# Zero products on TensorE in two places where it stands still, in an RWKV and SwiGLU block

## Chip, cores and metric

One core of one Trainium2 chip runs the kernel. The metric is the device time of one execution in microseconds. The kernel before takes 332.64 us (median of 3 runs).

## What is computed

The input x is 4096 steps of 256 channels, float32.

```python
xx = shift_by_one_step(x)
xk, xv, xr = (x * mix + xx * (1 - mix) for the three mixes)
k, v = xk @ Wk.T, xv @ Wv.T
rwkv = sigmoid(xr @ Wr.T) * wkv(-exp(time_decay), time_first, k, v)   # a recurrence over the steps
x = layernorm(x + rwkv @ Wo.T)
h = silu(x @ w_gate.T / 127) * (x @ w_up.T / 127)                     # 768 hidden, integer weights
x = layernorm(x + h @ w_down.T / 127)
```

## The kernel before, in words

The steps are cut into NC = 9 chunks, 0 to 8: 512 steps each, the first and the last 256. Channels lie on the partitions, in CH = 2 halves; the 768 hidden channels are NM = 6 tiles of 128. Work goes in rounds. Round j does the recurrence and the output product of chunk j, the projections K, V and R of chunk j+1, and the feed-forward of chunk j-1. Rounds 1, 2, 7 and 8 are written out, and rounds 3 to 6 are a hardware loop. The order on each engine is written out by hand, and engines wait for each other by semaphores.

TensorE's order in a round (`round_`, from L1038 on) is: gate and up products of chunk j-1 (`gate_up`, L1011, results in bank_a and bank_b), its down product (`down`, L1034, into bank_a), then the output product of chunk j (`attention_out`, L979, into bank_b), the projections K (bank_a) and V (bank_d) of the next chunk (`project`, L969), the transposes of x1 (`transpose_x1`, L988) and the projection R (bank_c). The feed-forward stands twice in the code, once for small and once for large weights, behind a branch on `any_wide`; only the first is run here, and the jump over the second comes right before the output product. In round 1 the projection V of chunk 2 comes earlier, in the middle of the down product of chunk 0. In round 8 the output product stands between the third and the fourth sixth of the down product of chunk 7, inside the branch.

`down` takes its six tiles in order. Tile m waits for `hhi` (ACT, L498) and `hlo`, the low part of the hidden tile; for tiles 0 to 3 POOL makes that (L344), for tiles 4 and 5 DVE (`low_part`, L763). DVE's order late in a round is: hidden products (L755), low part of tile 4, `gate_num` (L693), low part of tile 5, `divide` (L702, writes `rwkv` and lets the output product start), then `residual2` (L771) and its statistics (L709), then per half of the chunk the attention residual `res1` (L722, reads bank_b, so it waits for the output product) and statistics (L709), the means (L714), and the running maximum of the next chunk (L614).

`num_parts` counts `num_new` (L673), by which DVE has read V of chunk j from bank_d. From there on bank_d is free until the next V projection.

`keep_warm(bank, times)` (L941) multiplies a 128x128 tile of zeros with a 128x256 one and drops the result in the first 256 columns of a bank. The kernel before has it at the start (4 times), in round 0 (4 and 2 times, bank_a) and in round 8 (2 times, bank_c). A float32 product is two matmul records in the trace: `keep_warm(bank, 4)` is 8, and the output product of a full chunk (4 row blocks by 2 halves) is 16 at L979. A product in down's fp32r is one record.

Of the kernel before, what the change touches and what calls it, by code (L numbers as in the profile page):

```python
# [14 lines left out]
def rwkv_swiglu_kernel(nc: bass.Bass, xT: bass.AP, x: bass.AP, params: bass.AP, wk: bass.AP, wv: bass.AP,  # L15
# [14 lines left out]
    NM = H // P  # L30
# [19 lines left out]
    with ctx:  # L50
# [3 lines left out]
        def ps(name, shape):  # L54
            return ctx.enter_context(nc.psum_tensor(name, shape, f32))

        def sem(name):
            return ctx.enter_context(nc.semaphore(name))
# [74 lines left out]
        bank_d = ps("bank_d", [P, 2, N])  # L133
# [57 lines left out]
        num_parts = sem("num_parts")  # L191
# [36 lines left out]
        def first(c):  # L228

            return isinstance(c, int) and c == 0  # L230

        def last(c):
            return isinstance(c, int) and c == NC - 1

        def steps(c):

            return N // 2 if isinstance(c, int) and c in (0, NC - 1) else N
# [14 lines left out]
        def halved(c):  # L252

            return N // steps(c)
# [681 lines left out]
        def _(pe):  # L936
            def keep_warm(bank, times):


                for _ in range(times):  # L940
                    nc.tensor.matmul(bank[:, 0, 0:C], zeros[:, 0:P], zeros[:, :], start=True, stop=True)  # L941
# [29 lines left out]
                    mm.then_inc(ready, 1)  # L971

            def attention_out(c):
                pe.wait_ge(rwkv_ready, c + 1)
                if not first(c):
                    pe.wait_ge(hid_ready, c * NM)
                for q in range(steps(c) // P):
                    for h in range(CH):
                        mm = nc.tensor.matmul(attn[:, q, :], rwkv[:, h, q * P:(q + 1) * P], woT[:, h, :],  # L979
                                              start=(h == 0), stop=(h == CH - 1))  # L980
                    if q % 2 == 1:
                        mm.then_inc(attn_ready, halved(c))
# [33 lines left out]
            def down(c, tiles, full):  # L1016
                w = wd_f if full else wd_r
                if 0 in tiles:
                    if last(c):
                        pe.wait_ge(res2_ready, c * 2)  # L1020
                    else:
                        pe.wait_ge(act_ready, c * NM + NM)
                for m in tiles:
                    pe.wait_ge(hhi_ready, c * NM + (m + 1))
                    if m < NP:
                        pe.wait_ge(hlo_ready, c * NP + (m + 1))
                    else:
                        pe.wait_ge(hlo_last_ready, c * (NM - NP) + (m - NP + 1))
                    for q in range(steps(c) // P):
                        for part in (hhi, hlo):  # L1030


                            hp = part[:, m, q * P:(q + 1) * P]
                            mm = nc.tensor.matmul(ffn[:, q, :], hp.bitcast(f32) if full else hp, w[:, m, :],  # L1034
                                                  start=(m == 0 and q % 2 == 0 and part is hhi),
                                                  stop=(m == NM - 1 and part is hlo), skip_group_check=True)
                        if m == NM - 1 and q % 2 == 1:
                            mm.then_inc(ffn_ready, halved(c))  # L1038

            def ffn_products(j, full):  # L1040

                if full:
                    pe.wait_ge(ffn_w_f32_ready, 3)
                gate_up(j - 1, range(2), full)
                gate_up(j - 1, range(2, NM), full)
                if last(j):
                    down(j - 1, range(NM // 2), full)
                    attention_out(j)
                    down(j - 1, range(NM // 2, NM), full)
                elif isinstance(j, int) and j == 1:  # L1050
                    down(0, range(3), full)
                    project(2, V)
                    down(0, range(3, NM), full)
                else:
                    down(j - 1, range(NM), full)

            def round_(j, ffn, nxt):
# [9 lines left out]
                if not last(j):  # L1067
                    attention_out(j)
# [77 lines left out]
```

## Time and profile before

| | |
|---|---|
| runs, us | 332.36, 332.64, 334.7 |
| median, us | 332.64 |
| the profiled execution, us | 333.28 |
| its span in the profile, us | 331.4 |
| mean granted TensorE clock | 0.929 |
| PE busy | 286.2 us (86%) |
| DVE busy | 286.5 us (86%) |
| ACT busy | 215.5 us (65%) |
| POOL busy | 162.4 us (49%) |

The span runs from the first to the last instruction in the profile, and the time of the execution is 1.9 us longer. PE is TensorE's matmuls, PEld its weight loads. Matmuls are pipelined, so records of neighbours overlap: a matmul of a dense stream is shown longer than its distance to the next. The granted clock is a share of full speed (2.4 GHz). The rows speak of the executions' own time, in us from the start of the span.

### The profile page before, as it was taken

Reading aid. Unit: us, or ns where it says so; the run is one execution under the profiler, and the core shown is the slowest. Engines: PE = TensorE matmul, PEld = TensorE weight load, DVE = VectorE, ACT = ScalarE, POOL = GpSimd, SP = SyncE. Lnnn points to the kernel's source line nnn. Section 1 sums busy time; section 2 is a strip of 40 time slices with the busy share of each in tenths; the row PEclk is TensorE's granted clock in tenths of the full one; section 3 lists DMA queues with packets and bytes.
Section 4 is the critical chain, followed back from the end, with each engine's and each line's share of the span. In section 5 each row is a group of like instructions: output and inputs, shape, how many; then the busy total and the mean of one; then the engine's idle time right before and its main releaser. Section 6 shows DMA issues by size and latency. Waiting matters only on the chain.

```text
span 331.4 us, 4458 instructions
## 1 busy us (share of the span) xinstructions
PE 286.2 (86%) x1250; PEld 209.3 (63%) x1250; DVE 286.5 (86%) x484; ACT 215.5 (65%) x384; POOL 162.4 (49%) x125
## 2 busy tenths in 40 slices
PE   7686779999679994999969997999969995999892
PEld 5333666567655783747855677657855684868782
DVE  5999798899869989499888998999889998589764
ACT  3587467396816886088943888288934986099375
POOL 2567445407970199303991079703991099006030
PEclk9989679999969999699969999899979999899998
DMA  7701200400013010210104001030103010101002
GB/s 260 279 0 63 66 1 2 128 1 33 2 22 107 2 64 4 71 56 0 63 0 127 0 16 47 11 116 0 63 0 95 1 65 2 34 1 63 2 5 97
DMA packets 13527, 16.32 MB, mean 49 GB/s; under 512 B 704, under 2 KB 11200, under 8 KB 13504
## 3 DMA queue, kind: packets, MB, share of 16 engines
q1 hardware_dynamic: 12816, 15.48, 14.5%
q10 hardware_dynamic: 688, 0.53, 0.5%
q8 instruction: 15, 0.25, 0.3%
q14 instruction: 8, 0.07, 0.1%
HBM read 11.81 MB, written 4.19 MB: 48 GB/s over the span
## 4 chain that ended last, share of the span: by engine, by line
DVE 34%; PE 30%; issue 19%; ACT 13%; DVEq 1%; ACTq 0%
PE bank_b L979 12%; PE bank_b L1011 5%; DVE rwkv L702 5%; DVE hid L755 5%; PE bank_a L1011 5%; DVE wts L631 4%; DVE pmax L614 3%; ACT L514 3%; DVE state L660 3%; DVE state L648 2%; ACT den L454 2%; ACT den L460 2%; DVE gap L621 2%; PE bank_a L969 2%; DVE kv L654 2%
## 5 line engine op out<-in xcount | busy, mean ns | idle before, releaser
L344 POOL TENSOR_TENSOR hlo<-hid,hhi 128x512 fp32r<-128x512 f32 (+1 forms) x36 | 47.2, 1313 | 141.9 <-ACT hhi L498 141.9
L329 POOL TENSOR_TENSOR mix<-mix,xt 128x512 f32<-128x512 f32 (+1 forms) x46 | 59.9, 1333 | 9.3 <-ACT mix L424 9.3
L1034 PE MATMUL bank_a<-wd_r,hhi 128*128 128x256 f32 x192 | 48.8, 293 | 13.3 <-DVE hlo L763 13.3
L979 PE MATMUL bank_b<-woT,rwkv 128*128 128x256 f32 x128 | 40.8, 486 | 9.7 <-issue 6.9
L1034 PE MATMUL bank_a<-wd_r,hlo 128*128 128x256 f32 x192 | 47.4, 286 | 0.0
L1034 PEld LDWEIGHTS bank_a<-wd_r,hhi 128*128 128x128 f32 x192 | 36.9, 192 | 16.5 <-issue 15.6
L474 ACT ACTIVATE lnv<-mv,eps 128x4 f32<-128x4 f32 (+1 forms) x18 | 5.2, 290 | 58.7 <-DVE mv L714 58.7
L979 PEld LDWEIGHTS bank_b<-woT,rwkv 128*128 128x128 f32 x128 | 31.5, 253 | 17.9 <-issue 10.8
L498 ACT ACTIVATE hhi<-hid 128x512 fp32r<-128x512 f32 (+1 forms) x54 | 31.1, 578 | 11.2 <-DVE hid L755 11.1
L1034 PEld LDWEIGHTS bank_a<-wd_r,hlo 128*128 128x128 f32 x192 | 37.1, 193 | 0.3 <-issue 0.2
L416 ACT ACTIVATE wts<-wts 128x512 f32<-128x512 f32 (+1 forms) x54 | 28.1, 580 | 9.5 <-DVE wts L631 9.5
L1011 PE MATMUL bank_a<-x1hi,wg_r 128*128 128x512 f32 (+1 forms) x96 | 32.1, 414 | 1.5 <-ACT act L490 0.9
L424 ACT ACTIVATE mix<-dx,par 128x512 f32<-128x512 f32 (+1 forms) x46 | 28.6, 682 | 6.5 <-POOL dx L323 6.5
L490 ACT ACTIVATE act<-bank_a 128x512 f32<-128x512 f32 (+1 forms) x48 | 27.3, 568 | 7.0 <-PE bank_a L1011 6.4
L755 DVE TENSOR_TENSOR hid<-bank_b,act 128x512 f32<-128x512 f32 (+1 forms) x48 | 30.7, 642 | 1.3 <-PE bank_b L1011 0.6
L969 PE MATMUL bank_a<-mix,wkT 128*128 128x512 f32 (+1 forms) x64 | 28.9, 596 | 2.9 <-POOL mix L329 2.9
L1011 PE MATMUL bank_b<-x1hi,wu_r 128*128 128x512 f32 (+1 forms) x96 | 29.7, 391 | 1.5 <-DVE hid L755 1.5
L1011 PE MATMUL bank_a<-x1lo,wg_r 128*128 128x512 f32 (+1 forms) x96 | 29.7, 387 | 0.2
L1011 PE MATMUL bank_b<-x1lo,wu_r 128*128 128x512 f32 (+1 forms) x96 | 29.2, 386 | 0.0
L969 PE MATMUL bank_d<-mix,wvT 128*128 128x512 f32 (+1 forms) x64 | 27.2, 567 | 0.9 <-POOL mix L329 0.9
L969 PE MATMUL bank_c<-mix,wrT 128*128 128x512 f32 (+1 forms) x64 | 27.2, 566 | 0.0
L660 DVE TENSOR_TENSOR_SCAN state<-wts,state,kv 128x512 f32<-128x512 f32 (+1 forms) x18 | 26.3, 1466 | 0.0
(105 smaller groups left out, 581.6 us busy)
## 6 DMA issues: line engine op xcount, KB each, us to landing
xt<-xT SPq DMA_DIRECT2D x7, 513.0 KB, 3.9
xrow<-x SPq DMA_DIRECT2D x7, 512.0 KB, 3.9
out<-y SPq DMA_DIRECT2D x6, 512.0 KB, 2.8
wg_i<-wg SPq DMA_DIRECT2D x1, 768.0 KB, 8.9
wu_i<-wu SPq DMA_DIRECT2D x1, 768.0 KB, 10.3
wd_i<-wd SPq DMA_DIRECT2D x1, 768.0 KB, 12.0
out<-y SPq DMA_DIRECT2D x3, 256.0 KB, 2.1
xt<-xT SPq DMA_DIRECT2D x2, 257.0 KB, 3.1
```

The lines of the kernel that those rows point to most:

```text
L329: nc.gpsimd.tensor_tensor(mix[:, i, h, 0:n], mix[:, i, h, 0:n], xt[:, h, 0:n], ALU.add).then_inc(mixed, share(c, i, h))
L344: nc.gpsimd.tensor_tensor(hlo[:, m, 0:n], hid[:, m % NH, 0:n], hhi[:, m, 0:n].bitcast(f32), ALU.subtract).then_inc(hlo_ready, 1)
L416: nc.scalar.activation(wts[:, i, h, 0:n], wts[:, i, h, 0:n], ACT.Exp, scale=-1.0 if i == IN_OLD else 1.0).then_inc(wts_ready, 1)
L424: nc.scalar.activation(mix[:, i, h, 0:n], dx[:, h, 0:n], ACT.Copy, scale=par[:, MIX + i, h:h + 1]).then_inc(dx_scaled, share(c, i, h))
L490: nc.scalar.activation(act[:, m % 2, 0:n], gate_bank(c)[:, m % 2, 0:n], ACT.Silu, scale=SCALE).then_inc(act_ready, 1)
L498: nc.scalar.activation(hhi[:, m, 0:n], hid[:, m % NH, 0:n], ACT.Copy).then_inc(hhi_ready, 1)
L660: nc.vector.tensor_tensor_scan(state[:, 0, h, 1:n + 1], wts[:, IN_OLD, h, 0:n], kv[:, h, 0:n], state[:, 0, h, 0:1], ALU.mult, ALU.add).the ...
L755: nc.vector.tensor_tensor(hid[:, m % NH, 0:n], up_bank(c)[:, m % 2, 0:n], act[:, m % 2, 0:n], ALU.mult).then_inc(hid_ready, 1)
L969: mm = nc.tensor.matmul(bank[:, d, 0:n], w[:, h, d * P:(d + 1) * P], mixed_x[:, i, h, 0:n], start=(h == 0), stop=(h == CH - 1))
L979: mm = nc.tensor.matmul(attn[:, q, :], rwkv[:, h, q * P:(q + 1) * P], woT[:, h, :], start=(h == 0), stop=(h == CH - 1))
L1011: mm = nc.tensor.matmul(bank[:, m % 2, 0:steps(c)], w[:, h, m * P:(m + 1) * P], xp, start=(h == 0 and part is x1hi), stop=(h == CH - 1 and ...
L1034: mm = nc.tensor.matmul(ffn[:, q, :], hp.bitcast(f32) if full else hp, w[:, m, :], start=(m == 0 and q % 2 == 0 and part is hhi), stop=(m ...
```

## The change

`attention_out` of chunks 1 to 7 now first waits until bank_d is free and makes four zero products into it. `down` of chunks 1 to 7 does the same with three ahead of its last tile. Nothing is removed or moved.

```diff
             def attention_out(c):
+                if not first(c) and not last(c):
+                    pe.wait_ge(num_parts, c + 1)
+                    keep_warm(bank_d, 4)
                 pe.wait_ge(rwkv_ready, c + 1)
                 if not first(c):
                     pe.wait_ge(hid_ready, c * NM)
...
                 for m in tiles:
+                    if m == NM - 1 and not last(c) and not first(c):
+                        pe.wait_ge(num_parts, c + 2)
+                        keep_warm(bank_d, 3)
                     pe.wait_ge(hhi_ready, c * NM + (m + 1))
                     if m < NP:
                         pe.wait_ge(hlo_ready, c * NP + (m + 1))
```

## Rows read from the trace of the kernel before

**Rows 1.** The page, busy tenths and granted clock in 40 slices.

```profile
PE   7686779999679994999969997999969995999892
...
PEclk9989679999969999699969999899979999899998
```

**Rows 2.** Waits: engine, tile, line, whom for, us in total, times, longest.

```profile
PE bank_a L1034 <- DVE hlo L763: 13.3, 6, 2.8
PE bank_b L979 <- issue: 6.9, 3, 2.7
...
DVE res L722 <- PE bank_b L979: 16.7, 13, 3.3
```

**Rows 3.** Timeline of TensorE in round 4: start, duration, what, count, idle before.

```profile
165.47 0.28 PE L1034 MATMUL bank_a<-wd_r,hlo 128*128 128x256 f32 x1
168.01 0.36 PE L1034 MATMUL bank_a<-wd_r,hhi 128*128 128x256 f32 x1 [2.26 <-DVE hlo L763]
...
169.19 0.41 PE L1034 MATMUL bank_a<-wd_r,hlo 128*128 128x256 f32 x1
170.22 6.25 PE L979 MATMUL bank_b<-woT,rwkv 128*128 128x256 f32 x16 [0.61 <-DVE rwkv L702]
```

**Rows 4.** Timeline of DVE in round 4.

```profile
167.78 2.30 DVE L702 TENSOR_TENSOR rwkv<-num,den 128x1024 f32<-128x1024 f32 x1
...
171.21 1.39 DVE L709 BATCH_NORM_STATS2 stats<-res 128x6 f32<-128x256 f32 x4
...
174.83 0.75 DVE L709 BATCH_NORM_STATS2 stats<-res 128x6 f32<-128x256 f32 x2
176.51 0.69 DVE L722 TENSOR_TENSOR res<-bank_b,xrow 128x512 f32<-128x512 f32 x1 [0.92 <-PE bank_b L979]
```

**Rows 5.** Windows: stretch, length, busy of PE, PEld, DVE, ACT, POOL, clock, DMA.

```profile
170.22:175.30 5.08, 5.08 (x12) 4.09 (x13) 3.54 (x9) 0.30 (x1) 5.08 (x5) 0.50 0.00 0
...
308.61:310.25 1.64, 1.64 (x8) 1.46 (x9) 1.15 (x2) 0.20 (x1) 0.00 (x0) 1.00 0.00 0
```

**Rows 6.** Windows at the end of down, rounds 2, 7 and 4; last number GB/s.

```profile
90.50:91.70 1.20, 0.80 (x4) 0.51 (x3) 1.20 (x2) 1.20 (x3) 1.20 (x2) 0.50 0.05 14
...
278.80:280.30 1.50, 0.20 (x2) 0.00 (x0) 1.50 (x3) 0.47 (x2) 1.50 (x2) 1.00 0.05 11
169.20:170.20 1.00, 0.41 (x2) 0.11 (x1) 1.00 (x2) 1.00 (x3) 1.00 (x1) 0.50 0.00 0
```

**Rows 7.** Timeline of TensorE: down and output product of rounds 1 to 7.

```profile
56.34 0.28 PE L1034 MATMUL bank_a<-wd_r,hlo 128*128 128x256 f32 x1
57.11 3.72 PE L979 MATMUL bank_b<-woT,rwkv 128*128 128x256 f32 x16 [0.49 <-DVE rwkv L702]
...
93.09 5.56 PE L979 MATMUL bank_b<-woT,rwkv 128*128 128x256 f32 x16 [1.78 <-issue]
...
131.96 6.60 PE L979 MATMUL bank_b<-woT,rwkv 128*128 128x256 f32 x16 [2.67 <-issue]
...
205.93 0.40 PE L1034 MATMUL bank_a<-wd_r,hhi 128*128 128x256 f32 x1 [2.27 <-DVE hlo L763]
...
208.14 4.38 PE L979 MATMUL bank_b<-woT,rwkv 128*128 128x256 f32 x16 [0.32 <-DVE rwkv L702]
...
241.97 0.36 PE L1034 MATMUL bank_a<-wd_r,hhi 128*128 128x256 f32 x1 [2.27 <-DVE hlo L763]
...
242.88 0.28 PE L1034 MATMUL bank_a<-wd_r,hlo 128*128 128x256 f32 x1
244.19 5.11 PE L979 MATMUL bank_b<-woT,rwkv 128*128 128x256 f32 x16 [1.04 <-DVE rwkv L702]
...
281.48 5.25 PE L979 MATMUL bank_b<-woT,rwkv 128*128 128x256 f32 x16 [2.48 <-issue]
```

**Rows 8.** Timeline of TensorE at the end of down in round 8.

```profile
313.15 0.28 PE L1034 MATMUL bank_a<-wd_r,hlo 128*128 128x256 f32 x1
314.51 1.13 PE L941 MATMUL bank_c<-zeros 128*128 128x256 f32 x4 [1.08 <-issue]
```

## The prediction, made before the changed kernel was run

> **What bounds the kernel now.** I read the waits first, then one round in order of time, then the clock. The page's PEclk line shows what the change is aimed at: TensorE runs below full clock once in most rounds, though the PE line above it is nearly solid [rows 1]. The waits put two holes on TensorE: 13.3 us in 6 rounds ahead of the last sixth of the down product (for DVE's hlo, L763), and 6.9 us of "issue" in just 3 rounds ahead of the output product, L979. The reader is to see also whom this hurts: DVE waits 16.7 us in all for L979's bank_b [rows 2].
>
> Round 4 shows the mechanism. The first five sixths of down end at 165.6, the last eight matmuls come at 168.01 when hlo is there; the last of them takes 0.41 us, where the one before the hole took 0.28: the clock has fallen. rwkv is done at 170.08 (167.78 + 2.30), the output product starts at 170.22 and takes 6.25 us for 16 matmuls [rows 3, 4]. Its first twelve ran at granted clock 0.50, the lower level of 1.2 GHz, at 5.08/12 = 0.423 us each; eight in round 8 ran at 1.00 (2.4 GHz) in 1.64 us, 0.205 each [rows 5]. Round 1's sixteen took 3.72 [rows 7], so that is the full-clock price. DVE needs residual, statistics and one half of the attention residual first, and would be free for the second half at 171.21 + 1.39 + 0.69 + 0.75 = 174.04; it starts it at 176.51, when bank_b is complete [rows 4]. From there on TensorE is dense until five sixths of the next down, and DVE is dense beside it, so a later L979 makes the round later by as much: in rounds 4 to 6 the starts of L979 are 170.22, 208.14, 244.19, distances 37.92 and 36.05; the difference of 1.87 is that of the durations, 6.25 and 4.38 [rows 3, 7]. So what counts is **when the output product ends**, in rounds 1 to 7.
>
> **Rounds 2, 3 and 7** differ. There L979 starts 1.78, 2.67 and 2.48 us after TensorE fell idle, for "issue": nothing in the data is late [rows 7]. Just there stretches of 1.20 and 1.50 us hold DMA traffic of 14 and 11 GB/s, about 16 KB each (the first and the last of the three), while the same place of round 4 has 0 [rows 6]. These are the rounds written out (2 and 7) and the first pass of the loop (3); rounds 4 to 6, which run code that has been run, have none. I take the hole for instruction fetch at the jump over the unused branch of the product code. The new matmuls ahead of L979 stand behind that jump, so they can't run inside the hole. The Trainium skill, "Runtime: NRT & Kernel Launch", section "Instruction fetch mechanics", speaks against the change more strongly: code comes in blocks of 16 KiB, a taken branch to a block not held waits for it, and "The IRAM is only 2 cache lines". By that last sentence each pass of the loop would fetch too, rounds 4 to 6 would do as badly as 2, 3 and 7, and the sum below would be some 6 us higher, an estimate. The trace doesn't agree: in round 4 L979 follows rwkv by 0.14 us and nothing is fetched, so the rows decide.
>
> **The change, part by part.** Per product call keep_warm issues two matmuls: the four calls ahead of L979 are 8, the three ahead of the last sixth are 6. Price of one: L979's, same shapes. Eight cost 8 x 0.205 = 1.65, call it 1.7 us, at full clock and 8 x 0.423 = 3.4 us at half; six cost 1.3 or 2.5. The waits on num_parts are met early (num_new comes three hidden products before), so they cost nothing; queued behind them on TensorE is only what would wait for hlo or rwkv. bank_d is read by nobody then, except in round 1, where it already holds the next V; that alters values, not times. Each place in turn:
>
> Six ahead of the last sixth, rounds 2 to 7: they fill 1.3 us of holes of 13.3/6 = 2.2 us on average, so they end before hlo comes; cost 0. Where the cover is gone, in round 8, they cost their own time.
> In round 8 the last sixth of down(7) follows dense work and no hole is before it: TensorE goes from the last matmul at 313.15 to the old dummies at 314.51, again over an "issue" hole [rows 8]. Everything slides by 1.3. Bounds: 0 (if the slide is taken up by that hole) and 1.3; nearest is the second, since the jump itself comes later.
>
> Eight ahead of L979, **round 1**: last down matmul starts at 56.34, so dummies run from 56.46 to 58.16 [rows 7] and L979 starts at 58.16, not 57.11. The clock was full before. Loss 1.05, all visible, as DVE waits for L979 there.
>
> **Rounds 4 to 6.** Round 4: the last sixth starts at 168.01 and at full clock takes 1.03 (as in round 6, 241.97 to 242.88 plus 0.12); dummies to 170.74, 0.52 later than L979 starts now; L979 then takes 3.72 as in round 1 and ends at 174.46 instead of 176.47: gain 2.0. DVE's 174.04 is earlier, so it doesn't cut this. Round 5: 205.93 + 1.03 + 1.7 + 3.72 = 212.38 against 212.52: gain 0.15. Round 6: 241.97 + 6.45 = 248.42 against 244.19 + 5.11 = 249.30: gain 0.9. Sum 3.05. It rests on the clock staying full: the hole ahead of its fall in round 4 shrinks from 2.26 to about 1 us; if it fell all the same, see D.
>
> **Rounds 2, 3, 7**: L979 now starts at 93.09, 131.96, 281.48 and takes 5.56, 6.60, 5.25: 1.84, 2.88, 1.53 more than 3.72. At half clock half the time is lost, so it ran low for 3.7, 5.8 and 3.1 us. With the change dummies start at those times and 1.7 + 3.72 = 5.4 us of full-clock work follow. The hole between the last sixth and the dummies stays (1.8 to 2.7 us), so the clock can fall in it. Ends: clock full throughout, 5.4 each, changes of -0.15, -1.2, +0.15, sum -1.2; the same loss as now, 1.7 more each, sum +5.1. I take 2.8 us of low clock, a bit under the shortest of the three, since the six dummies ahead keep the clock up to the hole and the fall should come once and later: 5.4 + 1.4 = 6.8, changes +1.25, +0.2, +1.55, sum +3.0.
>
> Sum: +1.05 + 3.0 - 3.05 + 1.3 = +2.3 us. The profiled execution took 333.28 (span 331.4 and 1.9 around it), so 335.6; it stands 0.64 above the median of 332.64, which gives **334.9 us** as median, +0.7%. A measurement of this kernel tells about 1%, or 3.3 us, from no change.
>
> **Rivals.**
> A, slower: the clock loss in the fetch rounds stays whole. The place is the hole ahead of the dummies in rounds 2, 3, 7; the price 1.7 us each on top of today's; it decides once the low clock there lasts over about 4.5 us. Sum +1.05 + 5.1 - 3.05 + 1.3 = +4.4, median 337.0; were all three like round 3 (5.8 low), 8.3 each against 17.4 now, +7.5 and 339.4. For: the clock fell in or just after these holes each time. Against: the earlier hole is now filled.
> B: the clock stays full in all rounds but the dummies are still behind the fetch: +1.05 - 1.2 - 3.05 + 1.3 = -1.9, median 330.7. For: two thirds of the idle time ahead is filled. Against: 1.8 us and more stay empty.
> C, faster: the dummies hide in the issue holes, because the fetched block comes before them or the added code moves the jump targets so that the fetch is early. L979 starts as now and at full clock: -1.84 - 2.88 - 1.53 = -6.25 in place of +3.0, sum -6.95, median 325.7. Against: the jump precedes them, and moved targets can as well put a fetch where none is (round 1, about +2).
> D: it doesn't do what it says: zeros don't hold the clock, so rounds 4 to 6 stay low. Then 8 dummies of 3.4 us push L979 by 2 to 3 us each: about +7 in place of -3.05 on the forecast's sum, +12, median 344. Against: the kernel's own dummies of zeros are followed by full clock, as at 314.51, where four take 1.0 us up to the transposes.
>
> **Chances.** Forecast 0.52 (own range 333 to 336.5), A 0.23, B 0.13, C 0.09, D 0.03. The range 330.5 to 337.5 holds the forecast, B and most of A. Faster by over 1% (below 329.3): C and little else, 0.10. Slower by over 1% (above 336.0): A, D and the upper edge of the forecast, 0.28. Within 1%: 0.62.
>
> **What would show it.** Right: 14 more short matmuls on L941 per round, bank_d; rounds 4 to 6 have PEclk full from down through projection, L979 at 3.6 to 3.8 us, 35.7 us apart; DVE's wait for bank_b under 0.5 us there; in rounds 2, 3, 7 a hole of issue now in front of L941, and L979 starting 1.7 us or more after it; L979 of round 1 about 1 us later; transposes of round 8 1.3 us later relative to the output product. Wrong: L941 right behind the last sixth in rounds 2, 3, 7 with no hole (C); low clock in rounds 4 to 6 (D); L979 in the three fetch rounds at full clock (B) or at 6 us and more behind 3 us of dummies (A).

## The result, and the profile after

The changed kernel takes 336.42 us (median of 4 runs, 334.98 to 337.85) against 332.50 for the kernel before in the same comparison: a ratio of 1.012, 95% interval 1.008 to 1.016. It is slower, by 1.2%. The profiled execution took 335.70 us.

In round 1 the zeros land in bank_d while it holds V of chunk 2: the changed kernel computes with zeros in the first 256 steps of that V's first half, and so do the two runs below that keep these zeros (the output product alone, and all zeros without the branch). The same instructions run either way, but no run tests whether the values touch the times.

The granted clock of the changed kernel in 40 slices, from its page:

```profile
PEclk9899679999979999799999999999999998999998
```

Against [rows 1] the dips of rounds 4, 5 and 6 are gone. What was bought with it is in the waits:

```profile
DVE res L722 <- PE bank_b L982: 16.9, 9, 4.8
...
PE bank_d L941 <- issue: 6.6, 3, 2.2
...
PE bank_a L1040 <- DVE hlo L763: 5.4, 5, 1.5
```

The columns are those of [rows 2]. The wait for hlo fell from 13.3 to 5.4 us, as the zeros lie inside it. The three issue holes are all there, 6.6 us, now in front of the zeros (L941). And what counts up to round 8, DVE's wait for bank_b, is 16.9 us where it was 16.7 [rows 2]: fewer waits, but a longest of 4.8. (Lines move with the diff: L979 is now L982, L1034 is L1040.)

The timeline of TensorE, from the changed kernel. Round 1:

```profile
56.30 1.89 PE L941 MATMUL bank_d<-zeros 128*128 128x256 f32 x8
58.02 3.62 PE L982 MATMUL bank_b<-woT,rwkv 128*128 128x256 f32 x16
```

rwkv was done at 56.96 in this round (55.73 + 1.23). The output product waits for the zeros until 58.02. Round 4:

```profile
167.67 1.46 PE L941 MATMUL bank_d<-zeros 128*128 128x256 f32 x6
170.10 0.36 PE L1040 MATMUL bank_a<-wd_r,hhi 128*128 128x256 f32 x1 [0.97 <-DVE hlo L763]
...
171.09 1.89 PE L941 MATMUL bank_d<-zeros 128*128 128x256 f32 x8
172.81 3.62 PE L982 MATMUL bank_b<-woT,rwkv 128*128 128x256 f32 x16
```

This is the change as meant: 3.62 us for L982 where it was 6.25 [rows 3], at the price of a start 0.6 us behind rwkv. Rounds 5 and 6 look the same. Rounds 2, 3 and 7:

```profile
93.80 3.39 PE L941 MATMUL bank_d<-zeros 128*128 128x256 f32 x8 [2.20 <-issue]
97.03 3.62 PE L982 MATMUL bank_b<-woT,rwkv 128*128 128x256 f32 x16
133.52 3.13 PE L941 MATMUL bank_d<-zeros 128*128 128x256 f32 x8 [2.25 <-issue]
136.44 4.20 PE L982 MATMUL bank_b<-woT,rwkv 128*128 128x256 f32 x16
279.82 2.69 PE L941 MATMUL bank_d<-zeros 128*128 128x256 f32 x8 [2.15 <-issue]
282.30 4.66 PE L982 MATMUL bank_b<-woT,rwkv 128*128 128x256 f32 x16
```

In rounds 3 and 7 the product itself is a little longer too, 4.20 and 4.66 us. Two windows of round 2 tell where the low clock went there; the columns are those of [rows 5]:

```profile
93.80:96.60 2.80, 2.80 (x7) 2.26 (x8) 1.21 (x4) 0.00 (x0) 2.80 (x3) 0.50 0.02 6
97.03:100.40 3.37, 3.37 (x17) 2.98 (x16) 1.31 (x3) 0.00 (x0) 0.96 (x1) 1.00 0.29 77
```

The zeros ran at half clock and the output product at full clock. The zeros took the low clock in the product's place, at 3.2 us to save 1.9 ([rows 7], 5.56 against 3.62). Read in steps of half a microsecond, the granted clock is low for 3.4 us in each of the three rounds. In round 2 this starts in the hole, at 93.2; in rounds 3 and 7 only when zeros already run, at 134.2 and 281.0, and it reaches into the product.

The ledger by rounds: the start of DVE's second L722 of each round, which comes behind its waits for the output product, in both profiled executions, and by how much the distance from the entry above it grew.

| | before, us | after, us | grew by | forecast |
|---|---|---|---|---|
| round 1 | 60.87 | 61.67 | +0.80 | +1.05 |
| round 2 | 98.68 | 100.68 | +1.20 | +1.25 |
| round 3 | 138.60 | 140.68 | +0.08 | +0.2 |
| round 4 | 176.51 | 176.47 | -2.12 | -2.0 |
| round 5 | 212.56 | 212.25 | -0.27 | -0.15 |
| round 6 | 249.35 | 248.02 | -1.02 | -0.9 |
| round 7 | 286.76 | 287.00 | +1.57 | +1.55 |
| round 8, its only L722 | 310.74 | 310.96 | -0.02 | |
| round 8, transposes | 315.48 | 316.87 | +1.17 | +1.3 |
| end of the last instruction of DVE | 328.83 | 330.39 | +0.17 | |
| end of the span | 331.4 | 333.9 | +0.9 | |

Up to the L722 of round 8 the changed kernel is 0.22 us longer, which is about what DVE's wait for bank_b grew by (16.7 to 16.9). The transposes of round 8 add 1.17. The last two rows, +0.17 and +0.9, are outside the forecast: the products behind the transposes, which the change leaves alone, and the final store. So 1.4 of the 2.5 us between the two spans lie where the change acts.

### The profile page after: what moved, and what is told of

It is laid out like the page before. It is cut to its first block, busy times and chain, and to the rows that moved or that the text cites. A ratio compares the mean times of both kernels' runs of the same rounds, so it can differ in the third digit from the quotient of the medians.

```text
span 333.9 us, 4658 instructions
## 1 busy us (share of the span) xinstructions
PE 298.3 (89%) x1348; PEld 221.2 (66%) x1348; DVE 286.6 (86%) x484; ACT 215.2 (64%) x384; POOL 162.3 (49%) x125
## 4 chain that ended last, share of the span: by engine, by line
PE 36%; DVE 32%; issue 17%; ACT 11%; DVEq 1%; ACTq 0%
PE bank_b L982 7%; PE bank_b L1014 5%; PE bank_d L941 5%; PE bank_a L1040 5%; DVE hid L755 5%; PE bank_a L1014 5%; DVE wts L631 4%; DVE pmax L614 3%; DVE state L660 3%; DVE state L648 2%; ACT L514 2%; DVE gap L621 2%; PE bank_a L969 2%; PE bank_d L969 2%; DVE kv L654 2%
## 5 line engine op out<-in xcount | busy, mean ns | idle before, releaser
L1040 PE MATMUL bank_a<-wd_r,hhi 128*128 128x256 f32 x192 | 47.8, 289 | 5.5 <-DVE hlo L763 5.4
L1040 PE MATMUL bank_a<-wd_r,hlo 128*128 128x256 f32 x192 | 46.0, 279 | 0.0
L1040 PEld LDWEIGHTS bank_a<-wd_r,hhi 128*128 128x128 f32 x192 | 36.0, 188 | 9.9 <-issue 9.0
L1040 PEld LDWEIGHTS bank_a<-wd_r,hlo 128*128 128x128 f32 x192 | 36.1, 188 | 0.3 <-issue 0.2
L941 PE MATMUL bank_d<-zeros 128*128 128x256 f32 x98 | 26.9, 421 | 6.6 <-issue 6.6
L982 PE MATMUL bank_b<-woT,rwkv 128*128 128x256 f32 x128 | 30.8, 395 | 0.3 <-DVE rwkv L702 0.3
L982 PEld LDWEIGHTS bank_b<-woT,rwkv 128*128 128x128 f32 x128 | 25.7, 201 | 4.9 <-DVE rwkv L702 0.5
```

## The experiments

Each ran beside the kernel before, on one chip; the first three below and the one with four zero products ahead of the jump shared its runs (median 333.14 us), so did the last two (333.49), and so did the other four (333.59). Where two runs are compared, their ratios to the kernel before are the safer measure. In these texts "one branch" means that only the variant of the feed-forward that is run is left in the program, without the jump; the variant for large weights is missing.

### One place at a time

The zeros ahead of the last sixth alone:

```diff
             def attention_out(c):
-                if not first(c) and not last(c):
-                    pe.wait_ge(num_parts, c + 1)
-                    keep_warm(bank_d, 4)
                 pe.wait_ge(rwkv_ready, c + 1)
```

> The three zero products ahead of the last sixth stay, the four ahead of the output product go. Theory (the loss sits in the eight matmuls ahead of the output product wherever they start late: round 1 and the three rounds with an issue hole): the six matmuls lie inside the wait for hlo and cost nothing in rounds 2 to 7, the output product starts within 0.2 us of rwkv in rounds 4 to 6 and at full clock, round 8 still loses 1.2. Against the kernel before 330.5 us, 2 us faster (328.5 to 332), some 5 under the changed kernel. Rival (six matmuls are too few to hold the clock, and the gain of rounds 4 to 6 came from the eight): output product in rounds 4 to 6 at 4.4 to 6.3 us as before, time 333.5 to 334.

Measured: 331.65 us, ratio 0.995 (0.991 to 1.000). The output product of rounds 4 to 6 in that kernel:

```profile
169.59 5.40 PE L979 MATMUL bank_b<-woT,rwkv 128*128 128x256 f32 x16 [1.04 <-DVE rwkv L702]
...
206.67 3.72 PE L979 MATMUL bank_b<-woT,rwkv 128*128 128x256 f32 x16 [1.04 <-DVE rwkv L702]
...
242.06 3.71 PE L979 MATMUL bank_b<-woT,rwkv 128*128 128x256 f32 x16 [1.04 <-DVE rwkv L702]
```

In rounds 5 and 6 the product runs at full speed with the six matmuls alone; in round 4 it takes 5.40, so the clock still fell there. Of the rounds with an issue hole it is at full speed in round 7 (3.69 us) and not in rounds 2 and 3 (6.10 and 5.36). The time lies within the expected range, but the clock wasn't held in all of rounds 4 to 6 as expected. The first place is nearly free and a little good. The slower half of the change must be the other one:

```diff
                 for m in tiles:
-                    if m == NM - 1 and not last(c) and not first(c):
-                        pe.wait_ge(num_parts, c + 2)
-                        keep_warm(bank_d, 3)
                     pe.wait_ge(hhi_ready, c * NM + (m + 1))
```

> The four zero products ahead of the output product stay, the three ahead of the last sixth go. Theory: the hole ahead of the last sixth is open again, the clock falls as before in rounds 2 to 7, and eight matmuls at 0.42 us (3.4 us in all) stand in front of the output product: rounds 4 to 6 lose 1 to 3 us each instead of gaining; round 8 loses nothing. 338 to 341 us, slower than both kernels. Rival (the eight hold the clock by themselves, and the six only cost): output product at 3.6 us in rounds 4 to 6, 334 to 335 us.

Measured: 338.85 us, ratio 1.017 (1.007 to 1.027). Round 5 of that kernel:

```profile
208.55 0.38 PE L1037 MATMUL bank_a<-wd_r,hhi 128*128 128x256 f32 x1 [2.27 <-DVE hlo L763]
...
210.22 2.86 PE L941 MATMUL bank_d<-zeros 128*128 128x256 f32 x8
212.92 3.62 PE L982 MATMUL bank_b<-woT,rwkv 128*128 128x256 f32 x16
```

The hole of 2.27 us is back, the clock falls, and the eight zeros take 2.7 us up to the product. The product is then at full speed, but that is no gain: the low clock is served in front of it. DVE's wait for bank_b is 23.7 us. Round 4 of the same kernel is different: there the eight zeros ran at full clock without the six (1.7 us up to the product, which took 3.62). By the times the two places simply add up: 0.995 x 1.017 is 1.012, the ratio of the changed kernel. What the first does for the second shows in rounds 5 and 6, where the eight zeros take 1.7 us behind the six and 2.7 or 2.8 without them.

### What the issue holes are

```diff
             def round_(j, ffn, nxt):
                 if ffn:
-                    with pe.If(any_wide == 0):
-                        ffn_products(j, False)
-                    with pe.Else():
-                        ffn_products(j, True)
+                    ffn_products(j, False)
```

The last products, behind the rounds, are written once in the same way, and the load of `any_wide` goes.

> The kernel before, with TensorE's feed-forward products written once, without the branch on any_wide (the variant for large weights is left out; it is not run on these inputs). Theory (the issue holes of rounds 2, 3 and 7 are instruction fetch at the jump over the unused branch): they vanish, the output product follows rwkv by 0.1 to 0.3 us in all rounds, and the end comes 5 to 8 us earlier: 325 to 328. Rival (the hole is something else that comes with first-time code or with the product itself): holes of 1.8 to 2.7 us stay in rounds 2, 3 and 7, 332 to 333.

Measured, on the kernel without any of the new zeros: 325.96 us, ratio 0.975 (0.966 to 0.983). Its output products of rounds 2, 3 and 7:

```profile
92.19 5.39 PE L979 MATMUL bank_b<-woT,rwkv 128*128 128x256 f32 x16 [0.96 <-DVE rwkv L702]
...
129.24 5.40 PE L979 MATMUL bank_b<-woT,rwkv 128*128 128x256 f32 x16 [1.04 <-DVE rwkv L702]
...
277.35 3.72 PE L979 MATMUL bank_b<-woT,rwkv 128*128 128x256 f32 x16 [0.40 <-DVE rwkv L702]
```

No hole of issue is left: the idle time before them now ends with rwkv. The part of the page on DMA queues agrees, for the kernel before and for this one:

```profile
q8 instruction: 15, 0.25, 0.3%
```

```profile
q8 instruction: 6, 0.10, 0.1%
```

Nine packets of 16 KB less. The packets are counted for the whole program; with the traffic inside two of the holes [rows 6] they say that the holes are instruction fetch at the jump. Holes and the low clock behind them cost the kernel before some 7 us. With all zeros of the changed kernel on top of this edit:

> The changed kernel, with TensorE's feed-forward products written once (the variant for large weights is left out; it is not run on these inputs). Theory (without the jump there is no fetch hole, so the zero products do in all rounds what they do in 4 to 6): rounds 2, 3 and 7 have full clock throughout and L979 at 3.6 us about 0.5 us behind rwkv, rounds 1 and 8 lose 1 us each as before. 320 to 324 us; against the same kernel without zeros (325.96) 1 to 2% faster, where with the branch the zeros cost 1.2%. Rival (the eight matmuls cost their length wherever they stand, the fetch has no part in the loss): they again cost about as much as they bring, 326 to 330 us.

Measured: 321.28 us, ratio 0.964 (0.959 to 0.970). The same diff that costs 1.2% with the jumps brings 1.0% without them by the two ratios (0.964 against 0.975), or 1.4% by the medians, which are of different sets of runs (321.28 against 325.96). The two intervals just overlap, so the gain is likely and its size is not sure. Round 3 of this kernel is a good round, 0.6 us behind rwkv and at full clock:

```profile
127.21 1.89 PE L941 MATMUL bank_d<-zeros 128*128 128x256 f32 x8
128.93 3.62 PE L982 MATMUL bank_b<-woT,rwkv 128*128 128x256 f32 x16
```

### The same zeros on the other side of the jump

```diff
             def attention_out(c):
-                if not first(c) and not last(c):
-                    pe.wait_ge(num_parts, c + 1)
-                    keep_warm(bank_d, 4)
...
-                    if m == NM - 1 and not last(c) and not first(c):
+                    if m == NM - 1 and not last(c) and not first(c) and not last(c + 1):
...
                 else:
                     down(j - 1, range(NM), full)
+                    if not (isinstance(j, int) and j == NC):
+                        pe.wait_ge(num_parts, j + 1)
+                        keep_warm(bank_d, 4)
```

> The changed kernel with the four zero products at the end of the product code, ahead of the jump, in rounds 2 to 7 and not in round 1 (where V lies in bank_d), and without the three in round 8. Theory (the loss is where the dummies stand): in rounds 2, 3 and 7 they run inside the hole of the fetch, L979 starts about 3.5 us after the last sixth as in the kernel before and at full clock (3.6 us), rounds 1 and 8 lose nothing, rounds 4 to 6 gain as in the changed kernel. About 323 to 326 us, 2 to 3% faster than before. Rival (the fetch starts only when the dummies are through, so that the hole just comes 1.7 us later): L979 of rounds 2, 3 and 7 starts 5 us after the last sixth, at full clock, time about 328 to 330.

Measured: 324.93 us, ratio 0.973 (0.965 to 0.981). Round 3:

```profile
128.05 1.89 PE L941 MATMUL bank_d<-zeros 128*128 128x256 f32 x8
130.64 3.72 PE L979 MATMUL bank_b<-woT,rwkv 128*128 128x256 f32 x16 [0.71 <-issue]
```

The zeros run while the block is fetched, so the rival, a fetch that starts only when they are through, is out: of the hole, 0.71 us is left behind them (2.25 in front of them in the changed kernel), and after round 0 the clock doesn't fall until the products are through:

```profile
PEclk9989599999999999999999999999999999999997
```

With two products there instead of four:

> As the kernel with the zeros ahead of the jump (324.93), but with two products there instead of four. Theory (four matmuls of 0.85 us end before rwkv is done, so L979 of rounds 4 to 6 starts 0.1 us behind it instead of 0.5 later; DVE can't use much of that, as it is free for the first half only 2.6 us behind rwkv): 0 to 1 us faster, 324 to 325, if the clock holds. Rival (four are too few to hold the clock over the fetch hole): low clock in rounds 2, 3 or 7, 326 to 329 us.

Measured: 324.71 us, ratio 0.976 (0.970 to 0.982), no different. Four matmuls, with the six ahead of the last sixth, hold the clock over these holes too, in the one execution that was profiled:

```profile
127.83 1.03 PE L941 MATMUL bank_d<-zeros 128*128 128x256 f32 x4
130.62 3.71 PE L979 MATMUL bank_b<-woT,rwkv 128*128 128x256 f32 x16 [1.77 <-issue]
```

The zeros take 0.86 us less (1.03 against 1.89), but the product starts 2.79 us after their start, where it was 2.59: here the fetch decides when it starts, not the zeros.

### The two ends

```diff
-                if not first(c) and not last(c):
+                if not first(c) and not last(c) and not (isinstance(c, int) and c == 1):
...
-                    if m == NM - 1 and not last(c) and not first(c):
+                    if m == NM - 1 and not last(c) and not first(c) and not last(c + 1):
```

> The changed kernel without the four zero products of round 1 and without the three in round 8. Theory (terms of 1.05 and 1.2 us): DVE waits 0.7 instead of 1.6 us for L979 in round 1, the transposes of round 8 come 1.2 us earlier relative to L979 of that round; 2.2 us less than the changed kernel, 333.5 to 334.5 on its median, still no better than before. Rival (the ends of the kernel have slack, or the loss of the changed kernel sits elsewhere): 336 to 337 us as the changed kernel.

Measured: 335.06 us (median of 12), ratio 1.006 (1.003 to 1.009), so by the ratios 0.6%, or 2.0 us, better than the changed kernel; by the medians, of different sets of runs, 1.4. DVE waits 0.73 us in round 1 instead of 1.63. The two ends carry about half of the loss.

### Without the jumps, what are the two places worth?

Without the branch, with three zero products ahead of the last sixth, two ahead of the output product, and none in rounds 1 and 8:

> Products written once (the variant for large weights is left out), three zero products ahead of the last sixth and two ahead of the output product, none in rounds 1 and 8. Theory: all rounds at full clock, no hole but those for hlo and rwkv, nothing lost at the ends: 317 to 321 us, the fastest of all. Rival (DVE, dense behind rwkv, takes the place of TensorE and no more is to be had): as the run with one branch and all zeros.

Measured: 316.09 us, ratio 0.949 (0.944 to 0.954), the fastest, and a little below the expected range. In round 3 the product now follows rwkv:

```profile
126.28 1.02 PE L941 MATMUL bank_d<-zeros 128*128 128x256 f32 x4
127.48 3.71 PE L982 MATMUL bank_b<-woT,rwkv 128*128 128x256 f32 x16 [0.17 <-DVE rwkv L702]
```

DVE, on its timeline, no longer waits for it but for its own statistics:

```profile
128.47 1.39 DVE L709 BATCH_NORM_STATS2 stats<-res 128x6 f32<-128x256 f32 x4
130.15 0.69 DVE L722 TENSOR_TENSOR res<-bank_b,xrow 128x512 f32<-128x512 f32 x1 [0.30 <-DVE stats L709]
```

The same without any zeros ahead of the output product:

> As the run with one branch and two products (316.09; the variant for large weights is left out), without any zero product ahead of the output product: only the three ahead of the last sixth. It prices the second place alone where no fetch disturbs. Theory A (the six matmuls hold the clock in most rounds, as they did in rounds 5 and 6 of the first run): 316 to 318 us, the second place is worth under 0.5%. Theory B (both places are needed): low clock in several of rounds 2 to 7, L979 at 4.4 us and more, 319 to 322 us.

Measured: 318.76 us (318.05 to 322.92), ratio 0.957 (0.950 to 0.965). That is 2.7 us above the kernel with both places, between what theory A and B expect; without the one high run, 322.92, the median is 318.14 and the difference 2.0. The profile speaks for A: in rounds 2 to 7 the clock fell once, in round 2, whose second L722 starts at 97.48 instead of 95.98, most of the difference of the two profiled executions (318.14 and 316.42). How often it falls in the other executions isn't known. The high run was not profiled.

Last, a version that leaves nothing out. The branch stands once, around all rounds:

```diff
+            def rest(full):
+                round_(1, True, True, full)
...
+            with pe.If(any_wide == 0):
+                rest(False)
+            with pe.Else():
+                rest(True)
```

> The branch on any_wide stands once, around all rounds from the first (both variants of the program are there), with the zeros as in the run with one branch and two products. Theory (only the jumps inside the rounds cost): no issue hole ahead of L979, time within 1 us of 316.1, some 5% faster than before with nothing left out. Rival (a longer program or the branch itself costs): over 318 us.

Measured: 317.53 us (316.27 to 317.83), ratio 0.954 (0.948 to 0.960). It beats every other kernel here that has both variants of the products in the program. No issue hole stands ahead of L982 in its profile, though both variants are there: so it is the jump in each round that costs, and not the mere presence of the unused variant. It is 1.4 us above the run with one branch, a little more than I expected. What these are is open: the execution profiled, 316.27, was the fastest of the four and level with the profiled one of that run, 316.42.

## Why the prediction was right

The mechanism and its places were right. The closeness of the number, 335.6 us forecast for the profiled execution and 335.70 measured, is in part luck. The terms of the forecast add up to +2.3 us; in the ledger the same places give +1.4, and another 1.1 came from the products behind the transposes and the final store, which had no term. And by the median alone, 336.42, rival A (337.0) lies nearer than the forecast (334.9); it is the profile of one execution that decides between them. Point by point:

**The bound.** That only the end of the output product counts, one for one, held: in round 4 L982 is 2.63 us shorter (3.62 against 6.25) and starts 0.6 us behind rwkv instead of 0.14, which makes some 2.1, and the round is 2.12 us shorter; and where DVE gets free only after its half of the product has ended, as in the run with one branch and two products, its wait is gone.

**Rounds 4 to 6**, -3.05 forecast, -3.41 measured. Zeros hold the clock, so rival D is out. The eight matmuls delay L982 by 0.5 us as worked out (0.62 behind rwkv in round 4, where it was 0.14). The run with the six zeros alone shows that these hold the clock in rounds 5 and 6, but not in round 4.

**The fetch holes.** The hole stands in front of the zeros, so rival C is out for the changed kernel: the 6.6 us of issue in front of L941 show it. That the jump is the cause was an inference from 16 KB of traffic; the run with one branch shows it. What the Trainium skill, "Runtime: NRT & Kernel Launch", "Instruction fetch mechanics", says of jumps fits: without them no issue hole is left ahead of L979. Its sentence on two cache lines again doesn't: the loop's later passes, rounds 4 to 6, have no hole. (The same section gives TensorE 128 KiB, which is more than two blocks of 16; the prediction passed over that.)

**Rounds 2, 3 and 7**, +3.0 forecast, +2.85 measured. I had taken 6.8 us from the start of the zeros to the end of the product; in round 2 it is 6.85 (97.03 + 3.62 - 93.80), in round 3 7.12 (136.44 + 4.20 - 133.52), in round 7 7.14 (282.30 + 4.66 - 279.82). These 0.7 us too little were offset by something else that I had left out: counted from the ledger's entry of the round before, the zeros start 0.1, 0.4 and 0.3 us earlier than L979 did. Between rivals A (+5.1) and B (-1.2) the middle held because the clock fell once, in the hole or just behind it, and was low for 3.4 us, where I had taken 2.8; in round 2 some 0.5 of these lie in the hole, where they cost nothing. That length was a choice between two bounds, and other executions differ. In the profile of the kernel with rounds 1 and 8 spared, the same code in round 3 runs at full clock behind a hole of 2.55 us (1.83 us from the zeros to the product, which takes 3.62), as in rival B; in round 2 of it 7.9 us pass from the start of the zeros to the end of the product, more than A's 7.3 (5.56 + 1.7).

**Rounds 1 and 8**, +2.35 forecast, +1.97 measured, and their removal gives 2.0 us by the ratios and 1.4 by the medians.

**What was off** is the step from the profiled execution to the median: I took the profiled 333.28 to stand 0.64 us above the median of its kernel and used the same for the changed one. But the changed kernel's profiled execution lies 0.7 us below its median of 336.42, and so 334.9 was 1.5 us low. The runs of both kernels spread by about 3 us (331.42 to 334.7 and 334.98 to 337.85). Only the two kernels with one branch and zeros in both places lie within 1 us (320.63 to 321.46 and 315.73 to 316.42). A clock that falls in some executions and not in others, as just seen for round 3, would explain much of it, but the kernel with the zeros ahead of the jump spreads too (322.65 to 325.59), with no fall behind the start of round 1 in its one profile; what makes the spread is open.

## What to carry to other kernels

Filler matmuls can keep TensorE's clock if they run inside the hole. At its far end they ran at the low clock for the most part here, and lengthened the path by 2.5 to 3.2 us where the low clock had cost 1.5 to 2.9. So place them ahead of whatever makes the hole (a wait, or a jump whose target must be fetched), give them less time than the hole has, and leave out the rounds with no hole. And when the hole is a jump over code that is never run, take the jump out of the round first, by one branch around all rounds if both variants are needed: without the jumps the kernel was 7 us faster before a single new zero.

## What I had not expected of the hardware

A branch in each round, taken over an unused variant, left TensorE idle for 1.8 to 2.7 us in rounds 2, 3 and 7, where 0.4 to 1.0 is left without it, and the low clock came behind: 2.5% of the kernel. Round 1 runs its code for the first time too and shows no such hole (L979 starts 0.05 us behind rwkv); no run says why. Four matmuls of zeros, 1.0 us, ahead of a stretch with another 1.77 us of idle time, were enough, with the six ahead of the last sixth, to keep the granted clock at its upper level in the profile of that kernel, as good as eight.
